# A decoder kernel on one core: expert shares kept by group, expert, batch and token, and the output stored group by group

## The reference

```
x = x + self_attention(norm(x)); x = x + cross_attention(norm(x), ctx); x = x + mixture(norm(x))   # twice
```

```
probs = softmax(xf @ router_w); combine = the two largest probs of each token, in their columns
h = silu(einsum('nd,edf->nef', xf, w1)); routed = sum_e combine[:, e] * (h_e @ w2_e)
shared = sigmoid(xf @ shared_gate_w) * (silu(gate) * up @ shared_down)
return routed + shared
```

## Time and profile before

| | |
|---|---|
| median of 3 runs | 1337.83 us (1336.52 to 1340.89) |
| the profiled execution | 1335.68 us |
| its span | 1333.8 us |
| mean granted TensorE clock in it | 0.923 of full speed |
| experts of layer 0, group steps | from about 418 us |
| experts of layer 1, first load to router | from about 1151 us |
| group steps of layer 1 | 1186 to 1324 us, steady steps of 14.6 us |
| store stage | 1324 to 1333 us |

### The profile page before, as it was taken

The page is one execution under the profiler, slowest core; times in us unless marked ns, Lnnn a source line. Parts: engine busy times, 40 slices in busy tenths (PEclk is TensorE's granted clock), DMA queues, the critical chain, the costliest instruction groups (busy, mean ns, idle before and its releaser), DMA issues. The chain is left out here.

```text
span 1333.8 us, 33939 instructions
## 1 busy us (share of the span) xinstructions
PE 1162.1 (87%) x10468; PEld 816.1 (61%) x10468; DVE 965.4 (72%) x2103; ACT 753.9 (57%) x1729; POOL 648.7 (49%) x919
## 2 busy tenths in 40 slices
PE   4898988989876999999999688983999999748995
PEld 2555655656555777777777466662455555536774
DVE  5788888888843888878888477761577776437995
ACT  1577776667743555555555466651356665436773
POOL 8466576555542556666566111115455561314553
PEclk9999899999976999999999799995799999758998
DMA  6766687666402221212100000003755542025542
GB/s 157 168 127 118 126 163 161 129 130 125 101 10 60 74 64 64 64 64 64 59 4 1 0 1 0 1 1 73 139 103 115 107 93 68 2 61 179 179 157 63
DMA packets 88511, 112.57 MB, mean 84 GB/s; under 512 B 11761, under 2 KB 69393, under 8 KB 88385
## 3 DMA queue, kind: packets, MB, share of 16 engines
q1 hardware_dynamic: 82528, 105.02, 34.0%
q10 hardware_dynamic: 5856, 5.97, 1.7%
HBM read 88.09 MB, written 22.02 MB: 83 GB/s over the span
## 5 line engine op out<-in xcount | busy, mean ns | idle before, releaser
L1380 POOL TENSOR_TENSOR experts_shared_out<-experts_act_out,experts_share 128x512 f32<-128x512 f32 x136 | 188.5, 1386 | 139.8 <-ACT experts_act_out L1542 107.6
L1548 ACT CAST experts_hidden_hi<-experts_hidden 128x512 fp32r<-128x512 f32 x216 | 134.1, 621 | 122.6 <-DVE experts_hidden L1465 80.9
L687 DVE TENSOR_REDUCE heads_neg_max<-heads_ps_max 128x4 f32<-128x512 f32 x256 | 170.0, 680 | 43.0 <-PE heads_ps_max L845 40.8
L1484 DVE TENSOR_TENSOR experts_hidden_lo<-experts_hidden,experts_hidden_hi 128x512 fp32r<-128x512 f32 x184 | 199.2, 1083 | 1.3 <-ACT experts_hidden_hi L1548 1.1
L746 ACT ACTIVATE heads_E<-heads_ps_exp 128x512 f32<-128x512 f32 x256 | 150.5, 603 | 34.4 <-PE heads_ps_pv L867 28.8
L1542 ACT ACTIVATE experts_act_out<-experts_ps_gate 128x512 f32<-128x512 f32 x216 | 128.9, 598 | 70.7 <-PE experts_ps_gate L1596 68.5
L1465 DVE TENSOR_TENSOR experts_hidden<-experts_shared_out,experts_ps_up 128x512 f32<-128x512 f32 x136 | 92.0, 676 | 68.5 <-POOL experts_shared_out L1380 57.9
L687 DVE TENSOR_REDUCE cross_neg_max<-cross_ps_max 128x4 f32<-128x512 f32 x128 | 86.8, 685 | 59.3 <-PE cross_ps_max L845 58.7
L1594 PE MATMUL experts_ps_y<-experts_hidden_hi,experts_down_hi 128*128 128x512 f32 x216 | 95.1, 440 | 32.2 <-DVE experts_hidden_lo L1484 19.2
L845 PE MATMUL heads_ps_max<-QK 48*128 48x128 bf16 x1024 | 104.7, 228 | 18.5 <-DMA QK<-heads_qk_parts 14.4
L241 POOL TENSOR_TENSOR norm_var_eps<-norm_moments,norm_eps 128x2 f32<-128x2 f32 (+1 forms) x72 | 20.6, 285 | 185.7 <-DVE norm_moments L234 185.7
(11 more groups left out here) (230 smaller groups left out, 2944.6 us busy)
## 6 DMA issues: line engine op xcount, KB each, us to landing
experts_share<-experts_cT_dram SPq DMA_DIRECT2D x7, 2304.0 KB, 9.6
experts_share<-experts_cT_dram SPq DMA_DIRECT2D x7, 2048.0 KB, 9.0
heads_qk_parts<-heads_parts SPq DMA_DIRECT2D x32, 384.0 KB, 5.5
QK<-heads_qk_parts SPq DMA_DIRECT2D x64, 192.0 KB
QK<-heads_qk_parts SPq DMA_DIRECT2D x64, 128.0 KB
cross_qk_parts<-cross_parts SPq DMA_DIRECT2D x16, 384.0 KB, 4.7
QK<-cross_qk_parts SPq DMA_DIRECT2D x32, 192.0 KB
QK<-heads_qk_parts SPq DMA_DIRECT2D x64, 64.0 KB
```

Source lines behind the costliest of these rows:

```text
L687: nc.vector.tensor_reduce(neg_max[:, half, heads.start:heads.stop], ps_max[:, u % 2, :].rearrange("q (h k) -> q h k", h=HU), AX.X, ALU.max ...
L1380: nc.gpsimd.tensor_tensor(as_group(shared_out[c % 2][:]), as_group(act_out[b][:]), share[t.k % 2][:, :, row, :], ALU.mult).then_inc(weight ...
L1484: nc.vector.tensor_tensor(hidden_lo[b][:], hidden[b][:], hidden_hi[b][:].bitcast(F32), ALU.subtract).then_inc(lo_dve, 1)
L1548: nc.scalar.copy(hidden_hi[b][:], hidden[b][:]).then_inc(hi_ready, 1)
```

## The change

The layout of the shares is changed in `cT_dram` and in SBUF from (batch, expert, token) to (group, expert, batch, token). A share load of one group is one contiguous run for each partition in place of four. For that, `combine` is written in the order group, expert, batch, so that the transposes and the store to DRAM keep their number and size. The readers L1380 and L1476 index the buffer by row first.

The stage `store` is taken out. In the experts of layer 1 SP stores each group's four batches of x_sb when `x_added` says that they are added; these stores stand in SP's emit ahead of the share load of the same step. All of them are waited for at the end of the stage.

```diff
-        cT_dram = nc.dram_tensor(f"{name}_cT_dram", (B, SLOTS, S), F32).ap()
-        share = [sb(f"share{p}", [128, MG, rows, S]) for p in range(2)]
+        cT_dram = nc.dram_tensor(f"{name}_cT_dram", (NMG, SLOTS, MG, S), F32).ap()
+        share = [sb(f"share{p}", [128, rows, MG, S]) for p in range(2)]
         def load_share(sp, p, group):
-            sp.dma_start(share[p][:].rearrange("f b e t -> f b (e t)"),
-                         cT_dram[bass.ds(group, MG), 0:rows, :].rearrange("b e t -> b (e t)").partition_broadcast(128)
+            sp.dma_start(share[p][:].rearrange("f e b t -> f (e b t)").unsqueeze(1),
+                         cT_dram[bass.ds(group, 1), 0:rows, :, :].rearrange("g e b t -> g (e b t)").partition_broadcast(128)
                          ).then_inc(share_loaded[p], 16)
...
-        combine = spare[2][:, 0].rearrange("s (b e) -> s b e", e=SLOTS)
+        combine = spare[2][:, 0].rearrange("s (g e b) -> s g e b", e=SLOTS, b=MG)
...
-            sp.dma_start(cT_dram.rearrange("(q b) e t -> (b e) q t", q=4), combineT).then_inc(cT_stored, 16)
+            sp.dma_start(cT_dram.rearrange("(q a) e b t -> (a e b) q t", a=2), combineT).then_inc(cT_stored, 16)
             sp.wait_ge(cT_stored, 16)
             for these, semaphore in ((slice(0, HEAD_ROWS), share_head), (slice(HEAD_ROWS, rows), share_loaded[0])):
-                sp.dma_start(share[0][:, :, these, :], cT_dram[0:MG, these, :].partition_broadcast(128)).then_inc(semaphore, 16)
+                sp.dma_start(share[0][:, these].rearrange("f e b t -> f (e b t)").unsqueeze(1),
+                             cT_dram[0:1, these, :, :].rearrange("g e b t -> g (e b t)").partition_broadcast(128)).then_inc(semaphore, 16)
             def emit(t):
+                if is_last and t.has(1, NMG):
+                    sp.wait_ge(x_added, t.batch(1, 1))
+                    apart(sp, t, turns_sp)
+                    these = bass.ds(t.batch(MG, -MG), MG)
+                    sp.dma_start(out[these].rearrange("b s d -> s b d"), x_sb[:, these, :]).then_inc(x_stored, 16)
                 if t.has(0, NMG - 2):
                     p = (t.k + 1) % 2
                     if both:
                         need(sp, weighted, t.batch(len(both)))
                         apart(sp, t, turns_sp)
                     need(sp, hidden_ready, t.batch(C))
                     apart(sp, t, turns_sp)
-                    load_share(sp, p, t.batch(MG, MG))
+                    load_share(sp, p, t.batch(1, 1))
             pair_steps(sp, emit, FIRST, LOOP_FROM, LOOP_TO, LAST)
+            if is_last:
+                sp.wait_ge(x_stored, 16 * NMG)
...
-def store(nc, sem, out, x_sb):
-    with nc.Block() as block:
-        x_stored = sem("x_stored")
-        @block.sync
-        def _(sp):
-            sp.dma_start(out.rearrange("b s d -> s b d"), x_sb[:]).then_inc(x_stored, 16)
-            sp.wait_ge(x_stored, 16)
```

More of the change, by code:

```diff
@@ L1209, in pair_steps, with experts @@
         emit(Turn(None, k))
-def experts(nc, sem, name, x_sb, norm, ident, QK, w, matrices, layer):
+def experts(nc, sem, name, x_sb, norm, ident, QK, w, matrices, layer, out=None):
     sigmoid_top2, is_last = layer == 0, layer == 1
@@ L1297, in experts @@
         HEAD_ROWS = 2
-        share_head = sem("share_head")
+        share_head, x_stored = sem("share_head"), sem("x_stored")
         block = ctx.enter_context(nc.Block())
@@ L1379, in emit @@
                         need(pool, hidden_ready, t.batch(C, c + 1 - 2))
-                        nc.gpsimd.tensor_tensor(as_group(shared_out[c % 2][:]), as_group(act_out[b][:]), share[t.k % 2][:, :, row, :],
+                        nc.gpsimd.tensor_tensor(as_group(shared_out[c % 2][:]), as_group(act_out[b][:]), share[t.k % 2][:, row, :, :],
                                                 ALU.mult).then_inc(weighted, 1)
@@ L1408, in did @@
                 dve.wait_ge(route_step, step)
+            by_expert = combine[:, :, 0:EXP, :].rearrange("s g e b -> s g b e")
             def per_token(v):
@@ L1443, in _ @@
                 did(nc.vector.reciprocal(total[:], total[:]))
-                nc.vector.tensor_tensor(combine[:, :, 0:EXP], probs[:], per_token(total[:]), ALU.mult).then_inc(combined, 1)
+                nc.vector.tensor_tensor(by_expert, probs[:].rearrange("s (g b) e -> s g b e", b=MG),
+                                        total[:].rearrange("s (g b) -> s g b", b=MG).unsqueeze(3).to_broadcast([S, NMG, MG, EXP]), ALU.mult).then_inc(combined, 1)
             else:
-                nc.vector.tensor_tensor(combine[:, :, 0:EXP], probs[:], hit[:], ALU.mult).then_inc(combined, 1)
+                nc.vector.tensor_tensor(by_expert, *(v[:].rearrange("s (g b) e -> s g b e", b=MG) for v in (probs, hit)), ALU.mult).then_inc(combined, 1)
             dve.sem_inc(x_added, 1)
@@ L1475, in make_hidden @@
                     dve.wait_ge(act_ready, t.batch(C, c + 1))
-                    nc.vector.tensor_tensor(as_group(hidden[b][:]), as_group(act_out[b][:]), share[t.k % 2][:, :, row, :],
+                    nc.vector.tensor_tensor(as_group(hidden[b][:]), as_group(act_out[b][:]), share[t.k % 2][:, row, :, :],
                                             ALU.mult).then_inc(hidden_ready, 1)
@@ L1533, in _ @@
                 nc.scalar.activation(probs[:], others[:], ACT.Exp).then_inc(squashed, 1)
-                nc.scalar.activation(combine[:, :, EXP], logits[:, :, EXP], ACT.Sigmoid).then_inc(combined, 1)
+                nc.scalar.activation(combine[:, :, EXP, :], logits[:, :, EXP].rearrange("s (g b) -> s g b", b=MG), ACT.Sigmoid).then_inc(combined, 1)
             act.sem_inc(y_copied, 1)
@@ L1637, in _ @@
             for q in range(4):
-                last = nc.tensor.transpose(ps_cT[:, q, :], combine[:, 8 * q:8 * q + 8, :].rearrange("s b e -> s (b e)"), ident[:])
+                last = nc.tensor.transpose(ps_cT[:, q, :], combine[:, 2 * q:2 * q + 2].rearrange("s g e b -> s (g e b)"), ident[:])
             last.then_inc(cT_made, 1)
             pair_steps(pe, emit, FIRST + 1, LOOP_FROM, LOOP_TO, LAST)
-def store(nc, sem, out, x_sb):
-    with nc.Block() as block:
-        x_stored = sem("x_stored")
-        @block.sync
-        def _(sp):
-            sp.dma_start(out.rearrange("b s d -> s b d"), x_sb[:]).then_inc(x_stored, 16)
-            sp.wait_ge(x_stored, 16)
 def decoder(nc, a, out):
@@ L1683, in splits, with mixture @@
                     for i, (kind, n) in enumerate(counts(layer).items())]
-        def mixture(sem, layer, made):
+        def mixture(sem, layer, made, out=None):
             name = f"experts{layer}"
-            experts(nc, sem, name, x_sb, norm, ident, QK, {c: a[f"{name}_{c}"] for c in ("router", "router_bias", "rank")}, made, layer)
+            experts(nc, sem, name, x_sb, norm, ident, QK, {c: a[f"{name}_{c}"] for c in ("router", "router_bias", "rank")}, made, layer, out)
         sems = Semaphores(nc)
@@ L1712, in decoder @@
             sems.clear()
-            mixture(sems.stage("experts1"), 1, made)
-        store(nc, sems.stage("store"), out, x_sb)
+            mixture(sems.stage("experts1"), 1, made, out)
         sems.clear()
```

## The result

The changed kernel takes 1358.38 us (median of 4 runs, 1354.38 to 1371.75), the kernel before, measured beside it, 1339.36 us (1336.52 to 1342.08). The ratio is 1.016, with a 95% interval of 1.0086 to 1.0233: slower by 1.6%. The forecast was 1361.3 us, the stated range 1345 to 1377.

What follows compares the result with a forecast made beforehand. No engine was full over the span, but PE and DVE were nearly full in layer 1's steady step. Terms 40.8 - 10.6 - 6.7 = +23.5 us on 1335.68 gave 1359.2, 1361.3 for the median; range 1345 to 1377.

Steps and rivals of the forecast that it cites:

- The wait in SP's order: Layer 1's experts: share loads queued behind SP's wait for the addition stall DVE six times, 6.8 us each, +40.8 us.
- No catching up, and the clock: After each layer 1 stall: DVE regains nothing, PE's half-clock restart adds nothing, up to 1 us a step at most.
- The starts: Start of both layers' experts: faster head and rest transfers gain 4.6 us in layer 0, 6.0 in layer 1.
- pieces: Head transfers: four separate 1 KB pieces make them slow, so one 4 KB piece lands in 4.0 us, not 8.6.
- repeated reading: Head transfers: all partitions reading the same 4 KB is what is slow, so no gain there; chance 0.13.
- The end: After the last addition: a 256 KB store replaces 2048 KB, and the store stage's barrier goes, -6.7 us.
- The sum: Whole kernel: 40.8 - 10.6 - 6.7 = +23.5 us, 1361.3 us for the median.
- The slow head: Rival at both experts' starts: the head stays slow, the 10.6 us gain does not come, 1372 us; chance 0.13.
- DVE regaining the stall: Rival in layer 1's steps: DVE works off a backlog, each stall costs 3.4 us net, 1341 us; chance 0.08.
- loads landing at 7.1 us: Rival for layer 1's group loads: long runs keep 400 GB/s, stalls are 4.3 us, 1346 us; chance 0.11.
- the clock rival: Layer 1's stalls: PE's slow restart delays addition and next load, 1 to 2 us in six steps, about 1370; chance 0.07.

Runs made afterwards that it cites:

- the stores alone: The kernel before with its old layout, plus the change's per-group stores ahead of the share load, store stage removed: 1370.07 us, ratio 1.0236.
- both head experiments: Kernel before with head pieces 9 KB apart, 1338.77 us; the change with its head read as two transfers of two 1 KB pieces, 1357.71 us; single executions.

## Why the prediction was right

**The wait in SP's order, +40.8 forecast.** Right in place and mechanism, a little large in size. The six waits sum to 36.6 us, 6.1 each for 6.8. Of the terms, the distance from the addition's end to chunk 0 held (3.9 in the mean for 4.0). From the addition's end to the load's issue I had 0.6 us; it took 0.5 in the two steps written out and 1.1 to 1.3 in the four of the loop, 1.0 in the mean. From the issue to chunk 0 I had 9.6 + 0.6 = 10.2, the landing of the old layout and the store's transfer in front; it took 9.0. With the old layout, which the 9.6 were taken from, it took 9.7, so the store in front is worth about 0.1 there and not 0.6. That the stores alone gave 41.1 us of waits, nearly the forecast's 40.8, is in part luck: an issue that is 0.4 too short stands against a transfer that is 0.5 too long. In the change the shorter landing of the new layout comes on top. My sum left it out, since it took the landing from the old layout; hidden before the change, these loads no longer are.

**No catching up, and the clock.** From chunk 0 to the addition DVE took 11.2 us in the first step with a stall (1227.11 to 1238.29) and 10.5 in the last (1334.42 to 1344.89), 9.9 to 11.3 in the six and 10.7 in the mean, where the steady step has 10.0. It regained nothing there; it waited here and there for ACT and PE. PE, which stands still in a stall too, restarts at half clock after it, as the granted clock in this window of the changed kernel shows (us, then busy us and instructions of PE, PEld, DVE, ACT, POOL, then clock, DMA share and GB/s):

```profile
1271.70:1275.00 3.30, 3.22 (x8) 2.54 (x9) 3.30 (x5) 2.57 (x6) 1.53 (x1) 0.50 0.00 0
```

It begins 1.26 us after DVE's chunk 0; behind the other five stalls the same stretch has 0.50 four times and 0.55 once, and PE stands still for 5.7 us before this one. I had set this at nothing with up to 1 us at the top. The six steps are 40.4 us longer, of which 36.6 are share waits, so 3.7 us, 0.6 a step, are left for it and for what else delays DVE there; no run tells the two apart. This term was mis-sized, and the waits, 4.2 us too large, made up for it: 36.6 + 3.7 against 40.8. Behind the last stall 1.3 us come back, which I did not forecast: the last two additions lie 7.7 us apart in the change and in the stores alone, 9.05 in the kernel before, and DVE waits 2.38 us for PE there in place of 3.58. Why is not shown. That makes 39.1.

**The starts, -10.6 forecast.** Forecast 4.6 and 6.0, measured 4.4 and 7.0, together 11.4; the head lands in 4.6 where I had 4.0, the rest in 8.8 where I had 9.8. The choice between "pieces" and "repeated reading" was right. My word pieces was too loose: pieces of 1 KB are slow 8 KB apart, and fast 9 KB or 2 KB apart. The sentence from the Trainium skill, page "DMA: Bandwidth & Descriptors", section "Specifications", that 512 bytes are enough for line rate, stands better than I gave it: runs of 1 KB were fast in both head experiments. The same page of the Trainium skill, section "Latency and other measured facts", tells of row pitches at large powers of two that lower the rate of copies within HBM, and of a few KB of padding that restore it. Its pitches are from 512 KB up, ours is 8 KB, with all partitions reading the same rows. What is seen here is alike, head 8.6 us against 4.0 with 1 KB of padding, but nothing here shows that it is the same effect.

**The end, -6.7 forecast.** Measured 6.6; the last store lands in 2.3 us where I had 2.2.

**The sum, +23.5 forecast.** By these terms 39.1 - 11.4 - 6.6 = +21.1 us. The two spans differ by 22.8, with the 1.3 ahead of layer 0's store and another 0.4 between the two starts; the medians, 1358.38 and 1339.36, differ by 19.0.

**The rivals.** The slow head, DVE regaining the stall, and loads landing at 7.1 us did not occur; the clock rival occurred at 0.6 us a step in the mean at most, in place of 1 to 2.

## What to carry to other kernels

A queue that only issues transfers is still a program in order: before a wait is put into it, ask what stands behind, when that would have gone out, and who waits for it. Here one wait, harmless for its own store, moved six loads some 11 us later, past the 5.5 us by which they used to be early; with the load first the same change is 1.6% faster instead of 1.6% slower (1317.29 us, the best kernel here). When a transfer that many partitions read from the same rows is slow, look at the distance between the pieces too, and not at their length alone.

## What was not expected of the hardware

- Four pieces of 1 KB, 8 KB apart, read by all 128 partitions: about 80 GB/s, landing 8.6 us for 512 KB. The same pieces 9 KB apart: 4.0 us. The same number of bytes in 1 KB runs out of one contiguous 4 KB: DVE starts 5.25 us after the first issue, against 8.43. Why that distance is slow for such pieces stays open.
- Group loads of layer 0 land in 7.4 us with one run of 16 KB for each partition, in 9.0 with four of 4 KB that lie 8 KB apart, and in 8.5 with the same four 9 KB apart. So there the run length does seem to matter, 1.1 us of the 1.6. The first two figures come back in the other traces (7.1 to 7.4 us in the five kernels with the new layout, 8.9 in the stores alone), the 8.5 is of one execution. For layer 1's loads the same comparison, in kernels without stores beside them, gives 9.6 us before, 8.7 with 9 KB and 8.4 with the new layout.
